# Low-rank rows out of the value products: wider matmuls, values first in a pair, and a separate add on VectorE

## Chip, cores and metric

One NeuronCore of a Trainium2 chip runs the kernel. The metric is the device time of one execution, in microseconds; less is better. TensorE is called PE in the rows, VectorE DVE, ScalarE ACT, GpSimd POOL and SyncE SP.

## Reference, cut to what matters

```python
# x: (8, 256, 1024) fp32; LoRA rank R = 16, scaling 2
h  = x @ W.T + b + 2 * (x @ A[slot]) @ Bm[slot]        # per batch its own slot
q, k, v = h @ w_q, h @ w_k, h @ w_v                    # 32 query heads, 8 kv heads, head dim 32
o  = softmax(q k^T / sqrt(32)) v                       # each kv head serves 4 query heads
x  = x + o @ w_o
y  = x @ weight[id].T                                  # per batch its own 1024 x 1024
logits = y @ router_w.T;  gates = softmax of the top 2 of 4
x  = x + 4 * sum_e gates_e * (y @ A_e.T) @ B_e.T       # rank 16 each
```

## The kernel before

Precision: a product in fp32 is made of three matmuls in the format fp32r. Each operand is split into a high part (written by ScalarE as a rounded copy) and a low part (VectorE subtracts the high part from the original), and high x high, high x low and low x high are summed in PSUM.

Three stages follow one another, each with code for every engine.

The **fold** stage (`fold_stage`) multiplies W into the q, k and v weights, so that attention can be computed from x directly; the folded weights stand in `wq`, twelve blocks of 128 columns in the order of `BLOCKS`, high and low parts. It also folds the low-rank factor B and the bias into `b_scratch` and `bb_scratch`.

The **attend** stage (`attend_stage`) takes the batches in four **pairs**. A pair has 16 **steps** (`STEPS`), one for each kv head and batch, numbered n over all pairs (step 0 to 15 within one). In step n TensorE does, in this order: the scores of n, first two of four tiles (psS, L801); the work of **part 0**; outputs of n-3 (psO: probs times values at L825, row sums with p_sum at L829); the turning of the maxima (psM, L836); transposed scores of n-2, first two (psT, L812); the last two score tiles of n; the work of **part 1**; the last two transposed tiles of n-2. VectorE reduces each score tile to maxima (L673), splits them (L679, L681), and SyncE carries them as two rows into `q_stack`, where they are subtracted inside the transposed scores. ScalarE does the exps (L600), copies outputs (`o_sb`, L608) and GpSimd adds the two halves of probs into p_sum (L550).

The **work** is the projection of x into q, k and v. It fills the parts by a table written by hand, `WORK`; an entry such as `q3:0-4` is a **unit** and the range of 128-row tiles of x that it multiplies (three matmuls of 512 columns each, L759), and a + belongs to the next pair. A q or k unit ends with a low-rank matmul (L766) of `b_stack` with `u_stack`, which holds x times the low-rank factor A of each batch. That product is the unit `u`: 32 matmuls of 256 columns a pair (L740, L742), its parts added on VectorE and split. The value units v0 to v3 (one for each 128 tokens) have 24 matmuls of 256 columns (L774) and one low-rank matmul (L776).

The units go alternately into the two banks of `psP` in the order of `SEQ`. `free` makes a unit wait until the unit two before it has been read: by ScalarE (a q unit: four copies of 32 rows at L566; a value unit: one copy at L587) and by VectorE (a q or k unit: four subtractions, its lows, L653). In a step ScalarE works in the order: maxima rows, two exps, o_sb, units that ended in part 0, values that ended in part 1, two exps, splits of x, q or k units that ended in part 1. VectorE: two maxima, low parts of x (L432), units that ended in part 1 of the step before, two maxima and their split, units that ended in part 0. A q unit also needs its high rows doubled by a DMA (SyncE, L479) before its scores.

The x of the next pair is loaded in steps 11 and 12 as the last unit, q7, lets its tiles go (`x_used`), split by ScalarE in steps 11 (six tiles) and 12 (two), and by VectorE in steps 12 (six) and 13 (two).

The **finish** stage (`finish_stage`) multiplies by w_o and the second weight and computes the gated low-rank part. Its weights are loaded into blocks of `wq` during the last pair.

## Time and profile before

| | |
|---|---|
| median of 3 runs | 1053.18 us (1052.08 to 1053.78) |
| the profiled execution | 1050.59 us, span 1048.9 us |
| mean granted TensorE clock | 0.988 of full |
| TensorE busy | 1013.4 us, 97% |
| VectorE, ScalarE, GpSimd busy | 60%, 43%, 22% |
| fold, to the first value of attention | 0 to 162.5 us |
| a pair in the middle | 288.2 to 422.6 us |

The profiled execution is one run with its own time; the median is of other runs. A busy TensorE can still work at the lower of its two clock levels, so the granted clock is read beside the busy share.

### The profile page before, as it was taken

To read this page: it belongs to the slowest core of one execution; us is meant where nothing else is said; L and a number is where in the kernel's file an instruction comes from. 1 tells how busy PE (TensorE), PEld (TensorE's weight loads), DVE (VectorE), ACT (ScalarE), POOL (GpSimd) and SP (SyncE) were. 2 spreads that over 40 slices of the span, in tenths; PEclk is the share of its full clock that TensorE was granted. 3 is DMA by queue.
4 is the path that set the end of the run, shared out by engine and by line. 5 is a ranking of instruction groups with operands and counts; after the bars stand their busy time and mean duration, and the time that the engine had idled before them with its cause. 6 is when DMAs were issued, how large, how long until landed. Compare 5 with 4: busy or idle time off the path is not lost.

```text
span 1048.9 us, 17421 instructions
## 1 busy us (share of the span) xinstructions
PE 1013.4 (97%) x6934; PEld 820.2 (78%) x6934; DVE 633.5 (60%) x1071; ACT 449.5 (43%) x782; POOL 234.0 (22%) x224
## 2 busy tenths in 40 slices
PE   7999999999999999999999999999899999999997
PEld 6878787877678776787767787676589998988986
DVE  6562724667856578664776657654665655655653
ACT  5121223355754557554665556635422332323321
POOL 1000001123323233223332246643111111111100
PEclk9999999999999999999999999999999999999998
DMA  7030312111421124211232134453966756766531
GB/s 263 0 101 1 131 47 73 27 38 43 123 55 38 29 56 122 60 40 27 53 113 60 42 93 142 123 154 142 257 215 197 229 193 199 228 196 205 201 122 40
DMA packets 49888, 117.41 MB, mean 112 GB/s; under 512 B 7298, under 2 KB 26114, under 8 KB 45712
## 3 DMA queue, kind: packets, MB, share of 16 engines
q1 hardware_dynamic: 40080, 81.70, 26.4%
q0 software_dynamic: 9728, 34.61, 10.4%
q8 instruction: 55, 0.90, 0.4%
q14 instruction: 25, 0.20, 0.1%
HBM read 86.38 MB, written 18.89 MB: 100 GB/s over the span
## 4 chain that ended last, share of the span: by engine, by line
PE 90%; DMA 3%; DVE 3%; ACT 1%; SPq 1%; issue 1%; POOL 0%; ACTq 0%
PE psP L759 20%; PE psW L1043 17%; PE psF L254 11%; PE psG L1071 8%; PE psO L825 6%; PE psT L812 5%; PE psS L801 5%; PE psP L774 4%; PE psX L1286 3%; PE psO L829 2%; PE psY L1305 2%; PE psF L265 1%; DMA x_raw<-in_xT 1%; PE psM L836 1%; PE psP L740 1%; PE psP L742 1%
## 5 line engine op out<-in xcount | busy, mean ns | idle before, releaser
L673 DVE TENSOR_REDUCE nmax<-psS 128x2 f32<-128x512 f32 x256 | 164.5, 684 | 153.8 <-PE psS L801 152.1
L550 POOL TENSOR_TENSOR p_sum<-probs 128x512 f32<-128x512 f32 x128 | 167.6, 1310 | 372.6 <-ACT probs L600 372.3
L759 PE MATMUL psP<-x_hl,wq 128*128 128x512 f32 x960 | 235.1, 392 | 0.6 <-DVE q_stack L653 0.6
L759 PEld LDWEIGHTS psP<-x_hl,wq 128*128 128x128 f32 x960 | 175.2, 189 | 32.8 <-issue 0.8
L1043 PE MATMUL psW<-wq 128*128 128x256 f32 x1536 | 196.7, 283 | 1.6 <-DVE q_stack L653 1.2
L1043 PEld LDWEIGHTS psW<-wq 128*128 128x128 f32 x1536 | 190.3, 191 | 6.2 <-issue 1.3
L600 ACT ACTIVATE probs<-psT 128x512 f32<-128x512 f32 x256 | 139.2, 596 | 54.4 <-PE psT L812 53.9
L1052 ACT ACTIVATE cond_hi<-cond_raw 128x1024 fp32r<-128x1024 f32 x64 | 66.8, 1057 | 152.5 <-PE psG L1071 148.1
L1056 DVE TENSOR_TENSOR cond_lo<-cond_raw,cond_hi 128x1024 fp32r<-128x1024 f32 x64 | 78.3, 1235 | 89.1 <-ACT cond_hi L1052 89.0
L812 PE MATMUL psT<-q_stack,k_stack 98*128 98x512 f32 x256 | 90.1, 427 | 7.7 <-ACT probs L600 5.4
L653 DVE TENSOR_TENSOR q_stack<-psP,q_stack 32x512 fp32r<-32x512 f32 x128 | 87.8, 686 | 9.2 <-ACT q_stack L566 7.1
L801 PEld LDWEIGHTS psS<-k_stack,q_stack 96*128 96x128 f32 x512 | 80.0, 190 | 12.7 <-DVE nmax L673 1.1
L615 ACT ACTIVATE nmax_rows<-psM 16x128 f32<-16x128 f32 x64 | 17.1, 267 | 169.6 <-PE psM L836 169.6
L1003 POOL DMA_DIRECT2D cond_raw<-in_cond x64 | 33.8, 529 | 250.0 <-PE psG L1071 249.9
L801 PE MATMUL psS<-k_stack,q_stack 96*128 96x256 f32 x512 | 85.3, 287 | 0.1
L566 ACT ACTIVATE q_stack<-psP 32x512 fp32r<-32x512 f32 x128 | 75.2, 587 | 9.7 <-PE psP L766 8.1
L254 PE MATMUL psF<-q_hi,w_hi 128*128 128x512 f32 x184 | 72.0, 391 | 2.6 <-DVE bp L217 2.6
L254 PE MATMUL psF<-q_lo,w_hi 128*128 128x512 f32 x184 | 71.7, 389 | 0.0
L254 PE MATMUL psF<-q_hi,w_lo 128*128 128x512 f32 x184 | 71.6, 389 | 0.0
L825 PE MATMUL psO<-probs,v_sb 128*32 128x256 f32 x1024 | 69.3, 388 | 0.0
L812 PEld LDWEIGHTS psT<-q_stack,k_stack 98*128 98x128 f32 x256 | 43.0, 191 | 17.1 <-ACT probs L600 10.7
L825 PEld LDWEIGHTS psO<-probs,v_sb 128*32 128x32 f32 x1024 | 26.9, 110 | 31.5 <-issue 18.1
(122 smaller groups left out, 1252.8 us busy)
## 6 DMA issues: line engine op xcount, KB each, us to landing
cond_raw<-in_cond POOLq DMA_DIRECT2D x64, 512.0 KB, 4.1
x_raw<-in_xT SPq DMA_DIRECT2D x32, 256.0 KB, 3.9
q_stack<-q_stack SPq DMA_DIRECT2D x32, 256.0 KB, 3.1
o_scratch<-o_sb SPq DMA_DIRECT2D x64, 128.0 KB
o_raw<-rden_scratch SPq DMA_DIRECT2D x32, 256.0 KB, 5.4
o_raw<-o_scratch SPq DMA_DIRECT2D x8, 1024.0 KB, 8.8
x_sb<-in_xT SPq DMA_DIRECT2D x8, 1024.0 KB, 6.8
outT<-x_sb SPq DMA_DIRECT2D x32, 256.0 KB, 2.5
```

What stands on the lines that cost most here:

```text
L254: mm = pe.matmul(psF[:, bank(j, m)], w[:, k, m * P:(m + 1) * P], q[:, k], start=(k == 0 and i == 0), stop=(k == KT - 1 and i == 2))
L550: pool.tensor_tensor(p_sum[:, heads], probs[:, 0, heads], probs[:, 1, heads], ALU.add).then_inc(sum_done, 1)
L600: nc.scalar.activation(probs[:, i % 2, (i // 2) * 512:(i // 2 + 1) * 512], psT[:, i % 2], ACT.Exp, scale=ATT_SCALE).then_inc(exp_done, 1)
L653: ins = dve.tensor_tensor(to(h), both(psP[32 * h:32 * h + 32, bank(p, u)]), f(hi(h)), ALU.subtract)
L673: dve.tensor_reduce(nmax[:, n % 2, 2 * hp:2 * hp + 2, qt], psS[:, i % 2].rearrange("p (h k) -> p h k", h=2), AX.X, ALU.max, negate=True).t ...
L759: mm = pe.matmul(out, wq[:, i, w, k * P:(k + 1) * P], x[:, k, part], start=(k == 0 and n_ == 0), stop=False)
L801: mm = pe.matmul(psS[:, i % 2, j * T:(j + 1) * T], q_stack[0:96, slot, c, 2 * hp + j, qt * P:(qt + 1) * P], k_stack[0:96, c, g], start=Tru ...
L812: pe.matmul(psT[:, kt], k_stack[0:98, c, g, kt * P:(kt + 1) * P], q_stack[0:98, slot, c, 2 * hp:2 * hp + 2].rearrange("p h t -> p (h t)"), ...
L825: pe.matmul(psO[HD * h:HD * h + HD, 0], v_sb[:, c, kt, g], probs[:, kt, h * T:(h + 1) * T], start=(kt == 0), stop=(kt == KK - 1))
L1043: mm = pe.matmul(out, wq[:, k, w, m * P:(m + 1) * P], o_part(n % 2, o)[:, k], start=(k == 0 and i == 0), stop=(k == KT - 1 and i == 2))
L1056: dve.tensor_tensor(cond_lo[:, r % RAW], cond_raw[:, r % RAW], f(cond_hi[:, r % SPLIT]), ALU.subtract).then_inc(cond_lo_done, 1)
L1071: mm = pe.matmul(psG[0:EC, half], a[:, k], w[:, half * 512:(half + 1) * 512], start=(k == 0 and i == 0), stop=(k == KT - 1 and i == 2))
```

## The change

The factor A of both batches is put beside the value weights. `v_hi` is a new array whose 320 columns for each tile of x are: low and high part of A of batch 1, 256 value columns, high and low part of A of batch 0; `v_lo` holds the low parts of the value weights. A value matmul takes the value columns and the 32 columns of A of its own batch (288 columns; 272 for the low part of x, 256 for `v_lo`), so that the product of x and A falls out with tokens on the partitions. VectorE adds its two halves into `u_tok` (a reduce for each of v0 to v3), four transposes (unit `t`) turn it, and ScalarE and VectorE write `u_stack` from there. The unit u is gone.

The values must now come first in a pair, so the order of `SEQ` and the table change. The low-rank part of the values, which needs `u_stack`, becomes two units of two matmuls (`r0`, `r1`), which VectorE adds onto `v_sb` in SBUF. `v_sb` exists twice, since the values of a pair are written while the pair before still reads its own. Places in SBUF are moved, the last eight tiles of the fold are evacuated in two pieces, the loads of Wo come up to one step later, and the splits of x are shared out anew over the steps.

```diff
-BLOCKS = ["k0", "q0", "q1", "q2", "v0", "v1", "q3", "k1", "q4", "q5", "q6", "q7"]
+BLOCKS = ["k0", "q0", "q1", "q2", "q3", "k1", "q4", "q5", "q6", "q7", "v0", "v1"]
...
 WORK = [
-    (["v0"], ["q2:0-4"]),
-    (["q2:4-6"], ["q2:6-8"]),
-    (["v1"], ["v2"]),
-    (["v3"], ["q3:0-4"]),
-    (["q3:4-8"], ["k1:0-4"]),
-    (["k1:4-8"], ["q4:0-3"]),
+    (["r0", "r1"], ["q2:0-3"]),
+    (["q2:3-6"], ["q2:6-8"]),
+    (["q3:0-2"], ["q3:2-5"]),
+    (["q3:5-8"], ["k1:0-2"]),
+    (["k1:2-4"], ["k1:4-6"]),
+    (["k1:6-8"], ["q4:0-3"]),
     (["q4:3-6"], ["q4:6-8"]),
     (["q5:0-3"], ["q5:3-5"]),
-    (["q5:5-8"], ["q6:0-3"]),
-    (["q6:3-6"], []),
-    (["q6:6-8"], ["q7:0-3"]),
-    (["q7:3-6"], []),
+    (["q5:5-8"], ["q6:0-2"]),
+    (["q6:2-4"], ["q6:4-6"]),
+    (["q6:6-8"], ["q7:0-2"]),
+    (["q7:2-4"], ["q7:4-6"]),
     (["q7:6-8"], []),
-    (["+u:0-4"], ["+u:4-8"]),
-    (["+k0"], ["+q0"]),
-    (["+q1:0-4"], ["+q1:4-8"]),
+    (["+v0:0-4", "+v1:0-4"], ["+v0:4-8", "+v1:4-8"]),
+    (["+v2", "+v3"], ["+t", "+k0"]),
+    (["+q0"], ["+q1"]),
 ]
-SEQ = ["u", "k0", "q0", "q1", "v0", "q2", "v1", "v2", "v3", "q3", "k1", "q4", "q5", "q6", "q7"]
+SEQ = ["v0", "v1", "v2", "v3", "t", "k0", "q0", "q1", "r0", "r1", "q2", "q3", "k1", "q4", "q5", "q6", "q7"]
...
     def scalar(act):
...
+        def copy_t(p):
+
+            act.wait_ge(proj_done, unit(p, "t") + 1)
+            nc.scalar.activation(u_stack[0:32], psP[0:32, bank(p, "t")], ACT.Copy, scale=LORA_SCALE)
+            nc.scalar.activation(u_stack[32:64], psP[0:32, bank(p, "t")], ACT.Copy, scale=LORA_SCALE).then_inc(proj_act, 1)
...
-                for k in {11: range(0, 6), 12: range(6, KT)}.get(s, ()):
+                for k in {11: range(0, 3), 12: range(3, KT)}.get(s, ()):
                     split_x_hi(act, p + 1, k)
...
     def vector(dve):
...
+            if u[0] == "v":
+
+                c, rows = j // 2, NKV * (1 - j // 2)
+                dve.wait_ge(proj_act, act_unit(p, u) + 1)
+                if p and j == 0:
+                    dve.wait_ge(proj_done, unit(p - 1, "t") + 1)
+                dve.tensor_reduce(u_tok[:, j, c], psP[:, bank(p, u), rows:rows + 2 * R].rearrange("p (h r) -> p r h", h=2),
+                                  AX.X, ALU.add).then_inc(proj_dve, 1)
+            elif u == "t":
+                dve.wait_ge(proj_act, act_unit(p, "t") + 1)
+                dve.scalar_tensor_tensor(u_stack[64:96], psP[0:32, bank(p, u)], LORA_SCALE, f(u_stack[0:32]),
+                                         ALU.mult, ALU.subtract).then_inc(proj_dve, 1)
+            elif u[0] == "r":
+                values = v_sb[p % 2][:, j].rearrange("p k g d -> p (k g d)")
+                dve.wait_ge(proj_done, unit(p, u) + 1)
+                dve.wait_ge(proj_act, act_unit(p, f"v{2 * j + 1}") + 1)
+                dve.tensor_tensor(values, values, psP[:, bank(p, u)], ALU.add).then_inc(proj_dve, 1)
...
-                for k in {12: range(0, 6), 13: range(6, KT)}.get(s, ()):
+                for k in {12: range(0, 3), 13: range(3, KT)}.get(s, ()):
                     split_x_lo(dve, p + 1, k)
-            for unit_ in evacuated(n - 1, 1) if n else [(0, "q1")]:
-                if unit_[1] != "u":
+            for unit_ in finished(n - 1, 1) if n else [(0, "q1")]:
+                if unit_[1][0] in "qk":
+                    evacuate(*unit_)
+            for unit_ in finished(n, 0):
+                if unit_[1][0] not in "qk":
                     evacuate(*unit_)
...
     def tensor(pe):
...
+        def turn_rows(p):
+            free(p, "t")
+            pe.wait_ge(proj_dve, unit(p, "v3") + 1)
+            for t in range(TILES):
+                mm = pe.transpose(psP[0:32, bank(p, "t"), t * P:(t + 1) * P],
+                                  u_tok[:, t].rearrange("p c r -> p (c r)"), id_sb[:])
+            mm.then_inc(proj_done, 1)
...
+        def project_v(p, t, first, end):
+
+            c, toks = t // 2, slice(t * P, (t + 1) * P)
+            if first == 0:
+                free(p, f"v{t}")
+                if t == 0:
+                    pe.wait_ge(a_lo_done, p + 1)
+            out = psP[:, bank(p, f"v{t}")]
+            hi_rows, lo_rows, lo_out = ((slice(V0, VC), slice(V0, VC - R), slice(0, NKV + R)) if c == 0 else
+                                        (slice(0, VC - V0), slice(R, VC - V0), slice(R, NKV + V0)))
+            for k in range(first, end):
+                if t == 0:
+                    pe.wait_ge(x_lo_done, KT * p + k + 1)
+                pe.matmul(out[:, 0:NKV + V0], x[:, k, 0, toks], v_hi[:, k, hi_rows], start=(k == 0), stop=False,
+                          skip_group_check=True)
+                pe.matmul(out[:, lo_out], x[:, k, 1, toks], v_hi[:, k, lo_rows], start=False, stop=False,
+                          skip_group_check=True)
+                mm = pe.matmul(out[:, c * V0:c * V0 + NKV], x[:, k, 0, toks], v_lo[:, k], start=False, stop=(k == KT - 1),
+                               skip_group_check=True)
+            if end == KT:
+                mm.then_inc(proj_done, 1)
+
+        def low_rank_v(p, c):
+            free(p, f"r{c}")
+            for t in range(2):
+                toks = slice(c * T + t * P, c * T + (t + 1) * P)
+                mm = pe.matmul(psP[:, bank(p, f"r{c}"), t * NKV:(t + 1) * NKV], u_stack[:, toks],
+                               b_stack[:, VB * P:(VB + 2) * P], start=True, stop=True)
+            mm.then_inc(proj_done, 1)
```

On TensorE, at the start of pair 0: the last q unit (q1), the first scores, and what follows. Before:

```order
L766 MATMUL psP<-u_stack,b_stack 128x512
L801 MATMUL psS<-k_stack,q_stack 128x256 x4
L774 MATMUL psP<-wq,x_hl 128x256 x24
L776 MATMUL psP<-b_stack,u_stack 128x256
L801 MATMUL psS<-k_stack,q_stack 128x256 x4
L759 MATMUL psP<-x_hl,wq 128x512 x12
```

Now:

```order
L791 MATMUL psP<-u_stack,b_stack 128x512
L851 MATMUL psS<-k_stack,q_stack 128x256 x4
L819 MATMUL psP<-b_stack,u_stack 128x256 x4
L851 MATMUL psS<-k_stack,q_stack 128x256 x4
L784 MATMUL psP<-x_hl,wq 128x512 x9
```

The 24 matmuls of v0 stood between the two groups of scores; the four of r0 and r1 stand there now.

On VectorE, steps 12 and 13 of pair 0, from the first maxima of step 12 to the second of step 13. Before:

```order
L673 TENSOR_REDUCE nmax<-psS 128x2 [waits s_done] x2
L432 TENSOR_TENSOR x_hl<-x_raw,x_hl 128x512 [waits x_hi_done] x6
L673 TENSOR_REDUCE nmax<-psS 128x2 [waits s_done] x2
L679 CAST nmax_parts<-nmax 128x8 [waits s_max]
L681 TENSOR_TENSOR nmax_parts<-nmax,nmax_parts 128x8 [waits nmax_hi]
L653 TENSOR_TENSOR q_stack<-psP,q_stack 32x2x256 [waits half_hi]
L653 TENSOR_TENSOR q_stack<-psP,q_stack 32x2x256
L653 TENSOR_TENSOR q_stack<-psP,q_stack 32x2x256 [waits proj_act]
L653 TENSOR_TENSOR q_stack<-psP,q_stack 32x2x256
L673 TENSOR_REDUCE nmax<-psS 128x2 [waits s_done] x2
L432 TENSOR_TENSOR x_hl<-x_raw,x_hl 128x512 [waits x_hi_done] x2
```

Now:

```order
L703 TENSOR_REDUCE nmax<-psS 128x2 [waits s_done] x2
L452 TENSOR_TENSOR x_hl<-x_raw,x_hl 128x512 [waits x_hi_done] x3
L703 TENSOR_REDUCE nmax<-psS 128x2 [waits s_done] x2
L709 CAST nmax_parts<-nmax 128x8 [waits s_max]
L711 TENSOR_TENSOR nmax_parts<-nmax,nmax_parts 128x8 [waits nmax_hi]
L672 TENSOR_TENSOR q_stack<-psP,q_stack 32x2x256 [waits half_hi]
L672 TENSOR_TENSOR q_stack<-psP,q_stack 32x2x256
L672 TENSOR_TENSOR q_stack<-psP,q_stack 32x2x256 [waits proj_act]
L672 TENSOR_TENSOR q_stack<-psP,q_stack 32x2x256
L703 TENSOR_REDUCE nmax<-psS 128x2 [waits s_done] x2
L452 TENSOR_TENSOR x_hl<-x_raw,x_hl 128x512 [waits x_hi_done] x5
```

Three low parts of x have moved from ahead of q7's lows to behind them and behind the next maxima.

On TensorE, from part 1 of step 8 to part 0 of step 9 and its outputs (the step behind the end of q5). Before:

```order
L759 MATMUL psP<-x_hl,wq 128x512 x9
L812 MATMUL psT<-q_stack,k_stack 128x512 x2
L801 MATMUL psS<-k_stack,q_stack 128x256 x4
L759 MATMUL psP<-x_hl,wq 128x512 x9
L825 MATMUL psO<-probs,v_sb 32x256 x8
L829 MATMUL psO<-p_sum,ones 32x256 x4
```

Now:

```order
L784 MATMUL psP<-x_hl,wq 128x512 x6
L862 MATMUL psT<-q_stack,k_stack 128x512 x2
L851 MATMUL psS<-k_stack,q_stack 128x256 x4
L784 MATMUL psP<-x_hl,wq 128x512 x6
L875 MATMUL psO<-probs,v_sb_82 32x256 x8
L879 MATMUL psO<-p_sum,ones 32x256 x4
```

Both blocks of projection ahead of the outputs are six matmuls long instead of nine.

## Rows read from the trace of the kernel before

**Rows 1.** The page: its first line, and the busy time of each engine.
```profile
span 1048.9 us, 17421 instructions
PE 1013.4 (97%) x6934; PEld 820.2 (78%) x6934; DVE 633.5 (60%) x1071; ACT 449.5 (43%) x782; POOL 234.0 (22%) x224
```

**Rows 2.** Groups by line, whole run: busy us, mean ns, idle before.
```profile
L774 PE MATMUL psP<-wq,x_hl 128*128 128x256 f32 x384 | 48.6, 283 | 0.0
L587 ACT ACTIVATE v_sb<-psP 128x256 f32<-128x256 f32 x16 | 6.3, 395 | 8.1 <-PE psP L776 8.1
```

**Rows 3.** Chain of waits: start, us on the chain, what.
```profile
204.05 2.87 PE psP L774 x24
...
289.08 5.46 PE psP L759 x24
```

**Rows 4.** Waits of TensorE, 160 to 700 us: total, times, longest.
```profile
PE psT L812 <- ACT probs L600: 5.4, 3, 2.3
```

**Rows 5.** Timeline, TensorE, step 13 of pair 0: start, us, what.
```profile
286.11 0.28 PE L740 MATMUL psP<-x_hl,a_stack 128*64 128x256 f32 x1
...
287.96 0.64 PE L812 MATMUL psT<-q_stack,k_stack 98*128 98x512 f32 x2
```

**Rows 6.** Timeline, first scores of pair 0 and what follows.
```profile
183.53 0.71 PE L801 MATMUL psS<-k_stack,q_stack 96*128 96x256 f32 x4
...
184.04 1.29 DVE L673 TENSOR_REDUCE nmax<-psS 128x2 f32<-128x512 f32 x2 [2.15 <-PE psS L801]
...
185.36 2.79 DVE L653 TENSOR_TENSOR q_stack<-psP,q_stack 32x512 fp32r<-32x512 f32 x4
...
188.29 2.08 PE L759 MATMUL psP<-x_hl,wq 128*128 128x512 f32 x8 [0.58 <-DVE q_stack L653]
```

**Rows 7.** Timeline, steps 10 and 11 of pair 0; q6 has ended in step 10.
```profile
262.95 0.65 PE L801 MATMUL psS<-k_stack,q_stack 96*128 96x256 f32 x4
...
264.36 2.40 ACT L566 ACTIVATE q_stack<-psP 32x512 fp32r<-32x512 f32 x4
...
265.62 2.79 DVE L653 TENSOR_TENSOR q_stack<-psP,q_stack 32x512 fp32r<-32x512 f32 x4
...
266.79 1.09 ACT L600 ACTIVATE probs<-psT 128x512 f32<-128x512 f32 x2
...
267.95 1.28 POOL L550 TENSOR_TENSOR p_sum<-probs 128x512 f32<-128x512 f32 x1 [2.59 <-ACT probs L600]
...
268.57 1.07 PE L825 MATMUL psO<-probs,v_sb 128*32 128x256 f32 x16
...
269.46 0.61 PE L829 MATMUL psO<-p_sum,ones 128*32 128x256 f32 x8
...
270.04 0.71 PE L812 MATMUL psT<-q_stack,k_stack 98*128 98x512 f32 x2
...
270.59 0.65 PE L801 MATMUL psS<-k_stack,q_stack 96*128 96x256 f32 x4
...
271.20 0.19 PEld L812 LDWEIGHTS psT<-q_stack,k_stack 98*128 98x128 f32 x1 [0.18 <-ACT probs L600]
...
271.52 0.60 ACT L608 ACTIVATE o_sb<-psO 128x512 f32<-128x512 f32 x1
...
272.72 1.56 PE L759 MATMUL psP<-x_hl,wq 128*128 128x512 f32 x6
```

**Rows 8.** Timeline, VectorE, start of step 13 of pair 0.
```profile
283.35 1.29 DVE L673 TENSOR_REDUCE nmax<-psS 128x2 f32<-128x512 f32 x2
...
284.56 1.28 DVE L432 TENSOR_TENSOR x_hl<-x_raw,x_hl 128x512 fp32r<-128x512 f32 x2
```

**Rows 9.** The page, DMA issues: KB each, us from issue to landing.
```profile
q_stack<-q_stack SPq DMA_DIRECT2D x32, 256.0 KB, 3.1
```

**Rows 10.** Stretches: length, busy us by engine; last three: granted clock, DMA share, GB/s.
```profile
280.70:284.10 3.40, 3.40 (x25) 2.35 (x27) 3.33 (x6) 3.11 (x6) 1.21 (x1) 0.50 0.41 77
...
550.30:553.70 3.40, 3.40 (x23) 2.57 (x25) 3.30 (x6) 3.31 (x7) 0.99 (x1) 0.50 0.40 77
```

More of the change, by code:

```diff
@@ L65, in placer, with fold_stage @@
     return at
[L68 removed]
+def fold_stage(nc, sem, at, ctx, wq, v_hi, v_lo, id_sb, idx_sb, ones, W, Wqkv, bias, lora_BT, ident, idx, idx2_sb, idx2,
                b_scratch, bb_scratch):
@@ L318, in finished, with act_unit, attend_stage @@
     return [(p, u) for p, u, _, end in work(n, part) if end == KT]
-def evacuated(n, part):
-    if part:
-        return finished(n, 1)
-    late = [(p, u) for p, u in finished(n - 1, 0) if u == "v0"] if n else []
-    return late + [(p, u) for p, u in finished(n, 0) if u != "v0"]
 def unit(p, u):
     return NS * p + SEQ.index(u)
-def dve_unit(p, u):
-    return ND * p + SEQ_DVE.index(u)
-def attend_stage(nc, sem, at, ctx, wq, id_sb, idx_sb, ones, nmax, nmax_parts, before, ahead, xT, lora_A, b_scratch,
+def act_unit(p, u):
+    return NA * p + SEQ_ACT.index(u)
+def attend_stage(nc, sem, at, ctx, wq, v_hi, v_lo, id_sb, idx_sb, ones, nmax, nmax_parts, before, ahead, xT, lora_A, b_scratch,
                  bb_scratch, oT, den_scratch, rden_scratch):
@@ L395, in bank, with factor @@
         return unit(p, u) % 2
+    def factor(c, low):
+        i = (NKV + V0 + low * R) if c == 0 else (1 - low) * R
+        return slice(i, i + R)
     def pair_rows(scratch, p):
@@ L766, in project @@
                 pe.matmul(out, b_stack[:, i * P:(i + 1) * P], u_stack[:], start=False, stop=True).then_inc(proj_done, 1)
-        def project_v(p, t):
-            free(p, f"v{t}")
-            i = BLOCKS.index("v0")
-            out, toks = psP[:, bank(p, f"v{t}"), 0:NKV], slice(t * P, (t + 1) * P)
-            for k in range(KT):
-                for n_, (w, part) in enumerate(((0, 0), (0, 1), (1, 0))):
-                    pe.matmul(out, x[:, k, part, toks], wq[:, i:i + 2, w, k * P:(k + 1) * P],
-                              start=(k == 0 and n_ == 0), stop=False)
-            pe.matmul(out, u_stack[:, toks], b_stack[:, i * P:(i + 2) * P], start=False, stop=True).then_inc(proj_done, 1)
+        def project_v(p, t, first, end):
[18 more added lines that the diff above has]
+                mm.then_inc(proj_done, 1)
@@ L958, in ahead_sync @@
         if s == 8:
-            sp.wait_ge(before.proj_done, unit(PAIRS - 1, "q5") + 1)
+            sp.wait_ge(before.proj_done, unit(PAIRS - 1, "v3") + 1)
             for i in range(2):
```

234 lines of the change are left out of this document (113 added, 121 removed).

## Prediction, made blind

> **What bounds the kernel now.** I read the page first. TensorE is busy for 97% of the span [rows 1], so I take it as the bound and ask two things: what work of TensorE goes, and where TensorE will stand still that it did not before. The groups by line give the durations of one operation [rows 2], the chain of waits the true spacing of matmuls in a stream [rows 3], and the timeline shows, around four places, who waits for whom. The reader should see that TensorE works through its program almost without gaps: from 160 to 700 us its waits for ScalarE sum to 5.4 us [rows 4], all in one place, the end of a pair. The other engines lie close behind it, in places by only 0.2 us. So the order of the work counts as much as its amount.
>
> All times below are of the profiled execution, 1050.6 us with a span of 1048.9. The median of the runs is 1053.2, 2.6 above it, and I add that at the end.
>
> **The work that goes.** In a pair, 32 matmuls of the low-rank product (L740, L742) go. Sixteen take 1.85 us from the first to the score matmul behind them [rows 5], 0.116 each, so 3.7 us. The value products stay 24 to a tile, but 8 x (288 + 272 + 256) = 6528 columns instead of 6144. A run of 24 takes 2.87 us at 256 columns and 5.46 at 512 [rows 3]: 2.59 us for 6144 columns more, so 384 columns cost 0.16 us, and four tiles 0.65. Four transposes of 128 columns come in, at most 0.12 each by the 256-column spacing, 0.45. The four low-rank matmuls of the values only move. Sum: -3.7 + 0.65 + 0.45 = -2.6 us a pair, **-10.4 us** in four. New work of VectorE (four small reduces, two adds) and ScalarE (one copy less) counts only where TensorE waits for it.
>
> **Step 0 of every pair: r0, r1.** psP has two banks, and a unit may start when the unit two before it has been read. Before, v0 stood behind the first scores and needed only q0's bank; q2 needed q1's. The start of pair 0 shows what q1's bank costs [rows 6]: scores start at 183.53, VectorE's maxima at 184.04, q1's low parts follow until 188.15, and q2 starts at 188.29, 4.76 us after the scores. TensorE had 3 us of v0 in between and still waited 0.58. Now r1 needs q1's bank, and ahead of it stand only the scores (0.5) and r0 (0.25). It waits 4.76 - 0.75 = 4.0 us, four times, less the 0.6 of today: **+15.4 us**. Nothing can cover it: outputs, scores and q2 are queued behind r1.
>
> **Step 13: v0 waits for x.** VectorE now makes three of the low parts of x in step 12 and five in step 13 (six and two before), and v0:0-4 needs the first four. The fourth comes behind, on VectorE: maxima and their split, q7's four low parts, and the next two maxima. The pattern up to q7's lows is that of q6 [rows 7]: scores at 262.95, lows from 265.62 to 268.41, so +5.5 us. Two maxima take 1.3 [rows 8] and one x part 0.64 (two in 1.28, [rows 8]): +7.4. TensorE gets there earlier: from these scores to the next block of work are 2.1 us where nothing lies between (270.59 to 272.72, [rows 7]), and the nine matmuls on the first three tiles take about 1.1, so +3.2. The wait is 4.2 us, three times, 12.6. The data are not late: x's transfers start in step 11 as before. The 5.4 us of waits for ScalarE go [rows 4]: these were exps queued on ScalarE behind six splits of x, some of them waiting for a transfer, and now three splits stand there. **+7.2 us.**
>
> **Step 14: t waits for v3.** The transposes need v2 and v3 copied by ScalarE and reduced by VectorE. ScalarE comes to v2 only after the two exps and o_sb, which wait for the transposed scores: those start at 270.04, o_sb ends at 272.12 [rows 7], +2.1. Two copies of 0.395 us [rows 2] and a reduce of some 0.2 make +3.1; TensorE is free at +1.0, after the scores of 270.59. The wait is 2.1 us, three times. In pair 0 nothing stands ahead of the copy: 0.9. **+7.2 us.**
>
> **Step 15.** q0 ends one step later than before, and is doubled by a DMA that takes 3.1 us [rows 9]. ScalarE's copies begin 2.1 us after the transposed scores (behind o_sb), last 2.4 (264.36, [rows 7]), then the DMA: +7.6; TensorE, with q1 (5.7) between, is there at +7.2. 0.5 us, three times: **+1.5 us.**
>
> **Steps 4, 9, 11: the row sums.** These follow a step in which q3, q5 or q6 ends. The order is: four copies (264.36), then two exps (266.79), then GpSimd's sum until 269.23, which TensorE's matmul on p_sum needs; it started at 269.46, with 0.23 us to spare [rows 7]. From the scores of 262.95 that is 6.51 us, of which two blocks of 9 matmuls are 4.1. In the new table these blocks are 6 and 6, 1.37 us less. The chain over ScalarE and GpSimd keeps its 6.3 us, so TensorE waits 1.1 us, in part ahead of the probs matmuls. Three a pair, twelve in all: **+13.2 us.** In return parts 1 of steps 9 and 11, empty before, are filled, and the waits there of some 0.4 us (0.18 shown, and its like on the second tile, [rows 7]) go eight times: **-3.2 us.** Here is the surprise of the table: it spreads the work more evenly, and takes the reserve away where it was needed.
>
> **The clock.** The granted clock is 0.50, the 1.2 GHz level, for 3.4 us after the wait at each of the pair ends (280.7 the first, 550.3 the third) [rows 10]; such a stretch does 1.7 us of work, so it costs 1.7. Three in the transitions now. The new waits of 4.0 and 4.2 us are longer than any of these, so I give each a stretch (7), and the three of 2.1 two more: nine, six above today, **+10.2 us**. The Trainium skill ("TensorE: Matmul & The Clock Gate", section on HAM oscillation) says that a kernel whose matmuls are cut by waits pays the fall again at every one, "Every single K-tile". By it each of the ten new waits of 2 to 4 us would pay, seven above today, +11.9, a total 1.7 higher.
>
> **Sum:** -10.4 + 15.4 + 7.2 + 7.2 + 1.5 + 13.2 - 3.2 + 10.2 = +41.1 us, 1091.7 for a profiled execution, **1094 us** for the median.
>
> The fold stage pays nothing: its last eight tiles are copied and subtracted in two pieces, but v0 needs only tiles and x parts that VectorE has done before the bias matmul ends, give or take 0.5 us. The finish stage moves only addresses and one load of Wo.
>
> **Unknown costs.** The reduce of a 128x32 tile out of PSUM is not in the trace; it is 0.2 us if it is like the small ones, 0.68 if like a 128x512, which would add 0.5 to four waits: 0 to +2. The clock: with falls for the long waits only in part, +3; with one for every wait down to the 1.1 us, up to +25, though these are broken in two and shorter than anything that went with a fall. Row sums: 0 if ScalarE runs ahead, 13.2 if not, and in the last pair, where GpSimd splits Wo too, perhaps 3 more.
>
> **The rivals.** *Fewer waits than I count*: the clocks fall only as often as today and the row-sum waits vanish. For it: every row-sum chain has parts that could start sooner when TensorE has just been held up. Against: each of these chains starts at a matmul of TensorE itself, so lateness doesn't shorten it. -13.2 and up to -10.2: +18 to +28, 1071 to 1081.
>
> *Faster*: TensorE is the bound and arrives late everywhere, so the waits are covered as q2's nearly is today, where only 0.58 remains [rows 6]. Then -10.4, -3.2, the 5.4 us gone, and the three falls of the clock with them, 5.1: 24 us less, 1029. For it: the page's 97%. It decides once the new waits and their clock stay under 24 us together; I count 65. Against it: r1's is read off pair 0 almost directly, and alone with its clock it is 22. A partial form would end between 1045 and 1055.
>
> *Slower still*: SyncE or the transfers add a wait. The shortest steps now hold two blocks of 1.37 us, and in them the rows of the maxima must be copied, issued and landed (a q_stack transfer takes 3.1 us, [rows 9]) before the transposed scores. +5 to +15: 1099 to 1109.
>
> **The numbers.** My forecast (1084 to 1099) 0.5; fewer waits (1065 to 1084) 0.27; slower still 0.13; faster 0.06, a partial form near no change 0.04 (0.01 faster, 0.02 the same, 0.01 slower). A measurement of this kernel can tell 0.2%, 2.1 us. Range 1068 to 1103: it leaves out most of the last two and the end of slower still. Faster 0.07, same 0.02, slower 0.91.
>
> **What the new profile would show.** PE waits for DVE at the low-rank matmuls r1, four times 4 us; at the first 288-column matmul on the fourth x tile, three times some 4 us, with x_hl as releaser; at the transposes, three times 2 us; at p_sum, twelve times about 1 us with POOL or ACT as releaser. The value products 3.05 us for 24. The granted clock 0.5 in some nine stretches between 160 and 700. A pair of 134.4 us grows to about 145. Prediction wrong: if the r1 wait is under 1 us, VectorE gets to q1's lows in another order than I read; if p_sum never waits, the spare time is larger than the one place that I measured it at.

## The result and the profile after

The changed kernel takes **1102.05 us** (median of 4 runs, 1100.35 to 1103.01), against 1052.63 for the kernel before in runs beside it: a ratio of 1.047, 95% interval 1.0449 to 1.0491. The profiled execution took 1103.01 us with a span of 1101.2, 52.3 us above the span of [rows 1]. The forecast of 1094 was right in direction and 8 us low; the time lies 1 us inside the upper end of the range, 1103.

The page of the changed kernel, its first line and the busy time of each engine, against [rows 1]:

```profile
span 1101.2 us, 17254 instructions
PE 1021.1 (93%) x6822; PEld 818.7 (74%) x6822; DVE 637.4 (58%) x1099; ACT 448.4 (41%) x786; POOL 231.3 (21%) x224
```

TensorE runs 112 matmuls fewer and is busy 7.7 us longer, and its share falls from 97% to 93%. Both point the same way: less work, done in part at the lower clock, with more time standing still. No other engine grew by more than 4 us. The waits of TensorE from 160 to 745 us (what stood still <- what released it: us in total, times, longest), against [rows 4]:

```profile
PE psP L819 <- DVE q_stack L672: 15.3, 4, 3.8
PE psP L806 <- DVE x_hl L452: 12.0, 3, 4.0
PE psO L875 <- ACT probs L618: 11.6, 11, 1.8
PE psP L768 <- DVE u_tok L683: 6.2, 4, 1.8
PE psT L862 <- DMA q_stack<-nmax_rows: 5.4, 1, 5.4
PE psO L879 <- POOL p_sum L569: 3.6, 12, 0.5
PE psW L1094 <- DVE q_stack L672: 1.1, 1, 1.1
PE psS L851 <- issue: 1.0, 3, 0.4
```

L819 is r1, L806 v0's first product, L768 the transposes of t, L875 and L879 the output matmuls, L862 the transposed scores. All of these together are 56.2 us. In the kernel before, the same view down to the first psW matmul adds up to 10.6. The three waits that the change was predicted to bring to single places have their number and their size: four of 3.8, three of 4.0, three of 1.8 and one of 0.8.

How r1 comes to wait, in the timeline of all engines at the start of pair 1 (start, us, what; in brackets the idle time before it and its releaser):

```profile
335.44 0.71 PE L851 MATMUL psS<-k_stack,q_stack 96*128 96x256 f32 x4 [0.35 <-issue]
...
335.95 1.29 DVE L703 TENSOR_REDUCE nmax<-psS 128x2 f32<-128x512 f32 x2 [2.19 <-PE psS L851]
...
337.27 2.78 DVE L672 TENSOR_TENSOR q_stack<-psP,q_stack 32x512 fp32r<-32x512 f32 x4
340.09 0.69 DVE L693 TENSOR_TENSOR v_sb<-v_sb,psP 128x512 f32<-128x512 f32 x1
...
340.20 0.77 PE L819 MATMUL psP<-b_stack,u_stack 98*128 98x256 f32 x2 [3.81 <-DVE q_stack L672]
```

This is [rows 6] again, 152 us later: scores, maxima, q1's four low parts until 340.05, then r1 at 340.20, 4.76 us after the scores, as read blind from pair 0 of the kernel before. VectorE's own addition for r0 (340.09) starts after the parts of q1 and has nothing to do with the wait.

The wait that the prediction sized by the wrong rule is that of step 4, which stands four times in the row of L875. ScalarE and TensorE there, in pair 0:

```profile
219.62 0.60 ACT L626 ACTIVATE o_sb<-psO 128x512 f32<-128x512 f32 x1
221.21 2.41 ACT L583 ACTIVATE q_stack<-psP 32x512 fp32r<-32x512 f32 x4 [0.98 <-PE psT L862]
223.64 1.08 ACT L618 ACTIVATE probs<-psT 128x512 f32<-128x512 f32 x2
```

```profile
220.54 0.63 PE L862 MATMUL psT<-q_stack,k_stack 98*128 98x512 f32 x2
...
221.48 1.52 PE L784 MATMUL psP<-x_hl,wq 128*128 128x512 f32 x6
224.78 1.07 PE L875 MATMUL psO<-probs,v_sb 128*32 128x256 f32 x16 [1.77 <-ACT probs L618]
```

ScalarE has q3 to copy and stands idle for 0.98 us until transposed scores (L862, 220.54) have run. q_stack has three slots, and q3's is still being read by the scores of q0. Two exponentials are queued behind the four copies, and the outputs need them. From start to start the outputs are 1.84 us late here, and 0.72 us late in steps 9 and 11, where no copy waits for a slot: the difference, 1.1 us, is about the 0.98 us that ScalarE stood idle.

The granted clock in two stretches (length, PE busy, clock, DMA share, GB/s), against [rows 10]:

```profile
339.82:343.23 3.41, 3.03 (x26) 0.50 0.20 43
438.81:445.64 6.83, 5.55 (x35) 0.50 0.06 20
```

The first begins 0.38 us before r1 of pair 1 starts, near the end of its wait, the second 1.28 us before the end of the x wait of the next transition (435.80 to 440.09). From 160 to 745 us there are twelve such stretches with 54.6 us in all, where the kernel before has four of 3.4 us up to the same point. To price one, I took for each matmul in it the distance to the next start, less the median distance of the same two instructions at the full clock, and left waits out. A stretch of 3.4 us costs 1.1 to 1.7 us, one of 6.8 us 2.0 to 2.6. The twelve cost 20.6 us, the four before 5.9. These prices are estimates: with other groups of instructions for the medians the sums come out up to 1.3 us higher.

### The profile page after: what moved, and what is told of

Its sections match the earlier page's. It is cut to its first block, busy times and chain, and to the rows that moved or that the text cites. A ratio compares the mean times of both kernels' runs of the same rounds, so it can differ in the third digit from the quotient of the medians.

```text
span 1101.2 us, 17254 instructions
## 1 busy us (share of the span) xinstructions
PE 1021.1 (93%) x6822; PEld 818.7 (74%) x6822; DVE 637.4 (58%) x1099; ACT 448.4 (41%) x786; POOL 231.3 (21%) x224
## 4 chain that ended last, share of the span: by engine, by line
PE 84%; ACT 5%; DVE 5%; DMA 2%; POOL 1%; issue 1%; SPq 0%; ACTq 0%; DVEq 0%
PE psP L784 18%; PE psW L1094 16%; PE psF L274 11%; PE psG L1122 8%; PE psO L875 5%; PE psT L862 5%; PE psS L851 4%; PE psO L879 3%; PE psX L1337 3%; ACT q_stack L583 2%; ACT probs L618 2%; DVE q_stack L672 2%; PE psP L806 2%; PE psY L1356 2%; PE psP L808 1%; POOL p_sum L569 1%
## 5 line engine op out<-in xcount | busy, mean ns | idle before, releaser
L784 PE MATMUL psP<-x_hl,wq 128*128 128x512 f32 x960 | 245.8, 402 | 0.0
L784 PEld LDWEIGHTS psP<-x_hl,wq 128*128 128x128 f32 x960 | 179.6, 195 | 32.8
L862 PE MATMUL psT<-q_stack,k_stack 98*128 98x512 f32 x256 | 88.4, 425 | 5.4 <-DMA q_stack<-nmax_rows 5.4
L851 PEld LDWEIGHTS psS<-k_stack,q_stack 96*128 96x128 f32 x512 | 80.7, 193 | 14.5 <-issue 2.8
L875 PE MATMUL psO<-probs,v_sb 128*32 128x256 f32 x1024 | 73.6, 408 | 11.6 <-ACT probs L618 11.6
L875 PEld LDWEIGHTS psO<-probs,v_sb 128*32 128x32 f32 x1024 | 27.8, 114 | 46.1 <-issue 18.6
L862 PEld LDWEIGHTS psT<-q_stack,k_stack 98*128 98x128 f32 x256 | 44.1, 195 | 12.1 <-DMA q_stack<-nmax_rows 5.6
```

The lines of the kernel that those rows point to most:

```text
L784: mm = pe.matmul(out, wq[:, i, w, k * P:(k + 1) * P], x[:, k, part], start=(k == 0 and n_ == 0), stop=False)
L851: mm = pe.matmul(psS[:, i % 2, j * T:(j + 1) * T], q_stack[0:96, slot, c, 2 * hp + j, qt * P:(qt + 1) * P], k_stack[0:96, c, g], start=Tru ...
L862: pe.matmul(psT[:, kt], k_stack[0:98, c, g, kt * P:(kt + 1) * P], q_stack[0:98, slot, c, 2 * hp:2 * hp + 2].rearrange("p h t -> p (h t)"), ...
L875: pe.matmul(psO[HD * h:HD * h + HD, 0], v_sb[p % 2][:, c, kt, g], probs[:, kt, h * T:(h + 1) * T], start=(kt == 0), stop=(kt == KK - 1))
```

## The experiments

All are edits of the changed kernel, but for the sixth. Each was timed in three or five rounds beside the kernel before, which gave medians of 1054.34 (experiments 1 to 4), 1052.42 (5 to 8) and 1051.56 us (9 to 11). Since these shift by some us, gains that are added up are taken from the ratios. Spans are those of the profiled executions.

**1. r1 one part of a step later.**

```diff
-    (["r0", "r1"], ["q2:0-3"]),
+    (["r0"], ["r1", "q2:0-3"]),
```

> The changed kernel with r1 moved from part 0 of step 0 to part 1, ahead of q2; nothing else. My theory (each wait is a chain of its own that begins at a matmul of TensorE, so what is taken away comes back in full): outputs, transposed scores and two score tiles, some 2.5 us, now lie between r0 and r1 in three pairs, and only the score tiles, 0.5 us, in pair 0. The waits at the low-rank value matmuls fall from 15.3 us to about 8, with 2 to 3 us of the clock: 1092 to 1094 us against 1102. Rival theory (VectorE is the true limit around the start of a pair, and a wait that goes at one place comes back at the next): the wait moves to q2 or to the scores of step 1, and the time is 1099 to 1102.

1092.6 us (1090.1 to 1096.44), ratio 1.038 [1.034, 1.0421]. Waits of TensorE, 160 to 745 us:

```profile
PE psP L806 <- DVE x_hl L452: 12.0, 3, 4.0
...
PE psP L819 <- DVE q_stack L672: 5.4, 4, 2.4
```

9.9 us of the r1 wait are gone, and the time fell by 9.5, as expected. It did not come back as a wait at one place, which the rival needs: all waits in this view fell from 56.2 to 47.6 us. But the low clock up to the end of the pairs also costs some 5 us less, so the 9.5 (10.3 in the span) are less than the two together. Some 3 us did come back, about 1 of them as low clock in the last stage, the others in distances too short for the view of waits.

**2. Four parts of x in step 12.**

```diff
-                for k in {12: range(0, 3), 13: range(3, KT)}.get(s, ()):
+                for k in {12: range(0, 4), 13: range(4, KT)}.get(s, ()):
```

(and the same on ScalarE, one step earlier)

> The changed kernel with the splits of x shared out 4 and 4 over the two steps instead of 3 and 5, on ScalarE and VectorE; nothing else. My theory: v0:0-4 then has its four tiles before it starts; the wait for x_hl falls from 12.0 us to under 2, and the three falls of the clock behind it (4.4 us together) go too: 1086 to 1090 us. Rival theory (the time comes back at the next wait, since VectorE has the same work ahead of the second maxima of step 13): waits for x_hl or for the maxima in part 1 of step 13, 1097 to 1102 us.

1091.27 us (1088.96 to 1094.42), ratio 1.0369 [1.0332, 1.0407]. The row of x_hl, 12.0 us, is gone. In its place stands

```profile
PE psP L806 <- DVE q_stack L672: 5.0, 3, 1.7
```

which is v1, waiting for the bank of q7: 12.0 us given, 5.0 taken back, and the clock's share on top. The time is 1 us above the range that I had put on record.

**3. ScalarE copies the value tiles ahead of its exponentials.**

```diff
             more = n < N and p + 1 < PAIRS
+            for unit_ in finished(n, 0):
+                if unit_[1][0] == "v":
+                    evacuate(*unit_)
             if 1 <= n <= N:
                 act.wait_ge(turned, n)
...
             for unit_ in finished(n, 0):
-                evacuate(*unit_)
+                if unit_[1][0] != "v":
+                    evacuate(*unit_)
```

> The changed kernel with ScalarE copying v2 and v3 at the start of step 14, ahead of the maxima rows and the two exps instead of behind them and o_sb; nothing else. My theory: the copies are done while TensorE works on outputs, the wait at the transposes falls from 6.2 us to about 0.9 (pair 0 alone), and three falls of the clock (4.6 us) go: 1091 to 1094 us. Rival theory (ScalarE only shifts the delay to its exps): the transposed scores behind k0 wait instead, 1099 to 1102 us.

1093.53 us (1090.96 to 1095.05), ratio 1.0384 [1.0349, 1.0419]. The wait for u_tok falls from 6.2 us to 0.8, which is pair 0's alone. The other waits of the pairs stay; the last pair's wait for nmax_rows grows from 5.4 to 6.4 us.

**4. Parts of nine matmuls again.**

```diff
-    (["q3:0-2"], ["q3:2-5"]),
-    (["q3:5-8"], ["k1:0-2"]),
-    (["k1:2-4"], ["k1:4-6"]),
-    (["k1:6-8"], ["q4:0-3"]),
+    (["q3:0-2"], ["q3:2-4"]),
+    (["q3:4-6"], ["q3:6-8"]),
+    (["k1:0-2"], ["k1:2-5"]),
+    (["k1:5-8"], ["q4:0-3"]),
...
-    (["q5:5-8"], ["q6:0-2"]),
-    (["q6:2-4"], ["q6:4-6"]),
-    (["q6:6-8"], ["q7:0-2"]),
-    (["q7:2-4"], ["q7:4-6"]),
+    (["q5:5-8"], ["q6:0-3"]),
+    (["q6:3-6"], []),
+    (["q6:6-8"], ["q7:0-3"]),
+    (["q7:3-6"], []),
```

> The changed kernel with the table changed so that blocks of nine matmuls follow the end of q5 and of q6 as before the change, and q3 ends in part 1 of step 3 instead of part 0; parts 1 of steps 9 and 11 are empty again. My theory: TensorE's waits at probs and at p_sum (15.2 us) go nearly all, some 3 us of waits for exps in the two empty parts come back, 1 to 2 us of the clock go: 1087 to 1091 us. Rival theory (the waits at probs are set by the total of the work in a pair, not by where the blocks stand): at most 4 us, 1098 to 1102.

1092.32 us (1090.25 to 1093.18), ratio 1.037 [1.0337, 1.0402]. Of 15.2 us of waits for probs and p_sum 1.1 remain, while the wait for nmax_rows grows from 5.4 to 7.8 us; the time is 1 us above the expected range. But this edit does two things at once, and experiments 10 and 11 take them apart.

**5. Matmuls in place of the wait.** The kernel waits just as long for r1's bank, but TensorE is kept busy meanwhile. The result of the added matmuls is read by nothing.

```diff
         def low_rank_v(p, c):
+            if c == 1:
+                for i in range(32):
+                    pe.matmul(psM[:, P:P + NKV], wq[:, 0, 0, (i % KT) * P:(i % KT + 1) * P], v_lo[:, i % KT],
+                              start=True, stop=True)
             free(p, f"r{c}")
```

> The changed kernel, with 32 matmuls of 256 columns added ahead of the wait for r1's bank (their result, in a part of PSUM that nothing reads, is used nowhere, so they only keep TensorE busy for 32 x 0.12 = 3.8 us, about as long as the wait of 3.75 us). My theory: TensorE's idleness is what brings the stretches of 0.5 clock that follow r1 (starts at 196, 340, 490 and 637 us, costing 2.1, 0.24, 0.23 and 1.5 us of matmul time). r1 itself starts no later than now, those four stretches go, and the time falls by about 4 us, to 1098 us (1095 to 1101). Rival 1, the low clock follows from something else than the idle time (the place in the program, VectorE's or ScalarE's work): the stretches stay and the time is 1102 or, if the added matmuls run past the wait, some tenths per pair above. Rival 2, the whole excess over the waits (some 12 us) hangs on the first fall in each pair: the time falls by 8 us or more.

1093.71 us (1093.01 to 1096.73), ratio 1.0388 [1.0362, 1.0415]: 8.3 us less, twice what I expected. The timeline of TensorE in pair 1 and the clock of the stretch that holds the added matmuls (length, busy us of PE, PEld, DVE, ACT, POOL, clock, DMA share, GB/s):

```profile
331.99 0.40 PE L823 MATMUL psP<-b_stack,u_stack 98*128 98x256 f32 x2
332.23 4.00 PE L818 MATMUL psM<-v_lo,wq 128*128 128x256 f32 x32
336.21 0.47 PE L823 MATMUL psP<-b_stack,u_stack 98*128 98x256 f32 x2
```

```profile
333.50:336.90 3.40, 3.40 (x33) 3.02 (x36) 3.33 (x6) 0.75 (x2) 0.00 (x0) 1.00 0.36 77
```

From the second matmul of r0 to r1 are 4.10 us (332.11 to 336.21), and 4.09 without the added matmuls (336.11 to 340.20), so nothing was gained on the wait itself. No r1 is followed by a stretch of low clock any more, while in the changed kernel and in experiments 2, 3, 4, 10 and 11, which leave the wait of 3.8 us as it is, all four are. Of twelve stretches six are left, and their cost falls from 20.6 to 11.4 us, enough for the 8.3. The four stretches that follow an r1 cost 1.98, 1.12, 1.28 and 2.5 = 6.9 us, more than the 4.1 that I had put on record, since I had undercounted the output matmuls in them. Two more stretches (at 312.5 after the t wait of the first transition, and at 374.0 after a q3 wait, 2.9 us) didn't occur in this execution, and one after an x wait lasted twice as long, 1.1 us more. Of rival 2, that everything hangs on the first fall, no more than that is true: the x waits still fall, all three.

**6. The kernel before, with q6 and q7 in sixes.**

```diff
-    (["q5:5-8"], ["q6:0-3"]),
-    (["q6:3-6"], []),
-    (["q6:6-8"], ["q7:0-3"]),
-    (["q7:3-6"], []),
+    (["q5:5-8"], ["q6:0-2"]),
+    (["q6:2-4"], ["q6:4-6"]),
+    (["q6:6-8"], ["q7:0-2"]),
+    (["q7:2-4"], ["q7:4-6"]),
```

> The kernel before, with one part of the change done alone: q6 and q7 dealt out as two k-tiles per part of a step in steps 8 to 11, where it had three and then a part with none. My theory (the row sums' term of the prediction): with two k-tiles between them, TensorE reaches the output matmuls of steps 9 and 11 before the last exponentials of probs, 8 waits of about 1.1 us = 8.8 us, while the parts that no longer are empty give back about 3.2 us: 5.6 us more, ratio 1.005 (1.003 to 1.008), and waits for probs or p_sum rise from 6.5 to some 12 to 15 us. Rival 1, these waits in the changed kernel came from other work that moved with them: no change, ratio within 0.998 to 1.002. Rival 2, the clock falls at these waits as well: ratio above 1.009.

1052.22 us (1049.8 to 1054.9), ratio **0.9995** [0.998, 1.0011]. My theory expected 1.005 and missed. The waits did appear:

```profile
PE psO L825 <- ACT probs L600: 5.2, 8, 0.7
PE psT L812 <- ACT probs L600: 4.4, 3, 1.6
PE psO L829 <- POOL p_sum L550: 3.1, 10, 0.6
```

and they have the predicted size. One place, in pair 0:

```profile
268.29 1.07 PE L825 MATMUL psO<-probs,v_sb 128*32 128x256 f32 x16 [0.65 <-ACT probs L600]
269.65 0.64 PE L829 MATMUL psO<-p_sum,ones 128*32 128x256 f32 x8 [0.28 <-POOL p_sum L550]
```

The view has 0.65 and 0.28 us; from start to start, against the usual distances, it is 0.72 and 0.46, 1.18 together, where 1.1 was forecast. What the prediction sized too low is what the filled parts give back. The starts of the psM transposes, one a step, tell the net price of this dealing. They are subtracted here from one another for pair 2, from step 8 on:

```
                 turn to turn, us             sum of four
before           7.64  5.87  7.64  5.86       27.01
in sixes         7.49  6.50  7.49  6.50       27.98
```

That is 0.97 us a pair, 3.9 in four. Two waits of 1.18 are 2.36 a pair, so the filled parts give back 1.4, where the forecast had 0.8. Against the 3.9, this execution has two stretches of low clock in place of four up to the end of the pairs, 3.3 us less. Whether that is the new dealing or chance stays open: over all runs the mean granted clock is 0.9886 (12 runs) against 0.9867 (18 runs of the kernel before), some 2 us, which is not clear of their scatter. What the runs bound is the whole: at most 1.2 us more.

**7. r0 and r1 where their bank is long free.** q2 goes ahead, and both low-rank products use q1's bank, with counters of their own; q3, the next unit of that bank, waits for the second addition.

```diff
-    (["r0", "r1"], ["q2:0-3"]),
-    (["q2:3-6"], ["q2:6-8"]),
+    (["q2:0-2"], ["q2:2-4", "r0"]),
+    (["q2:4-6", "r1"], ["q2:6-8"]),
...
-            free(p, f"r{c}")
+            if c:
+                pe.wait_ge(low_added, 2 * p + 1)
+            else:
+                pe.wait_ge(proj_act, act_unit(p, "q1") + 1)
+                pe.wait_ge(proj_dve, unit(p, "q1") + 1)
...
             if first == 0:
                 free(p, u)
+                if u == "q3":
+                    pe.wait_ge(low_added, 2 * p + 2)
```

> The changed kernel, with the two low-rank products of the values put where the bank they write is long free: q2 goes ahead of them, r0 in the second part of step 0 and r1 in the first part of step 1, both in q1's bank, with counters of their own. My theory: the r1 wait (15.3 us over four pairs) goes altogether, not just the 9.9 us of the first experiment, and with it the 4 us of low clock that follow it: 1085 us (1081 to 1090), and the largest waits left on psP are u_tok's 6.2 and x_hl's 12.0. Rival, VectorE's lateness (the copies of q1 and q2 and the added sums stand in the same row) only shows up at the next bank, q3's, or at the outputs of step 3: 1090 us or more, with a wait at q3 or ahead of the outputs of some 1 to 2 us each.

1078.61 us (1076.81 to 1081.02), ratio 1.023 [1.0204, 1.0255]. Waits of TensorE, 160 to 748 us:

```profile
PE psP L809 <- DVE x_hl L453: 12.0, 3, 4.0
...
PE psP L826 <- DVE q_stack L673: 0.8, 1, 0.8
```

23.4 us less for one edit: 14.5 of the r1 wait (0.8 remain, at r0 of pair 0), 7.6 of the clock (20.6 to 13.0). That is 2.4 us beyond the low end of what I expected, and again the clock was worth more than I had put on it.

**8. All four repairs (edits 2, 3, 4 and 7).**

> The changed kernel with all four repairs at once: r0 and r1 apart, x_hl in four and four, the copies of v ahead of the exponentials, and the parts of nine matmuls. My theory (the losses are separate waits that add up): 1102 less 17, 11, 8.5 and 10 = about 1055.5 us (1050 to 1061), ratio to before 0.998 to 1.008; waits left inside the pairs: q7's bank ahead of v1 (5.0) and the last pair's nmax_rows (5 to 8). Rival 1, the change's saving of 10.4 us comes through once its waits are gone: 1040 to 1047 us, ratio 0.988 to 0.995. Rival 2, the repairs overlap (each removes a bit of the same lateness): 1062 us or more, ratio above 1.009.

1046.25 us (1045.91 to 1051.83), ratio **0.994** [0.992, 0.9961]: 0.6% below the kernel before. My estimate (1050 to 1061) missed; the time lies in the range of rival 1. Waits of TensorE, 160 to 748 us, those of the pairs:

```profile
PE psT L873 <- DMA q_stack<-nmax_rows: 5.5, 1, 5.5
PE psP L813 <- DVE q_stack L677: 5.2, 3, 1.8
PE psT L873 <- ACT probs L619: 1.6, 2, 1.3
PE psW L1105 <- DVE q_stack L677: 1.2, 1, 1.2
PE psO L890 <- POOL p_sum L570: 1.1, 1, 1.1
PE psS L862 <- issue: 1.0, 3, 0.4
PE psP L830 <- DVE q_stack L677: 0.8, 1, 0.8
PE psP L773 <- DVE u_tok L688: 0.8, 1, 0.8
PE psS L862 <- DVE nmax L708: 0.7, 2, 0.5
```

They sum to 17.9 us, 7.3 above the kernel before. The low clock up to the end of the pairs costs 3.7 against 5.9 there, 2.2 less. With the -10.4 of work that the prediction counted, this makes -5.3 us. Its span is 1044.2, 4.7 below [rows 1]. So the balance closes with the work at the figure that was counted, within 1 us.

**9. The last pair's transfers.** Experiment 8, with o_raw's 1 MB from o_scratch issued a step later than the four transfers of rden_scratch.

```diff
-        sp.dma_start(o_land(n % 2), oT[n]).then_inc(o_landed[n % 2], 16)
+        if n:
+            sp.dma_start(o_land(n % 2), oT[n]).then_inc(o_landed[n % 2], 16)
...
             load_o(sp, 0)
+        if s == 9:
+            sp.dma_start(o_land(0), oT[0]).then_inc(o_landed[0], 16)
```

> The kernel with all repairs (1046.3 us), with one change of the last pair's transfers: o_raw's 1 MB from o_scratch is issued one step later than the four transfers of rden_scratch, and not right behind them. My theory: the rows of nmax that TensorE waits 5.5 us for in the last pair (2.3 in the kernel before) land late because 2 MB of o_raw stand on the 16 engines ahead of them; with half of it a step later that wait shrinks to 0 to 2 us and the 6.8 us stretch of low clock that follows it (2.2 us) goes: 1039 to 1042 us, ratio to before 0.988 to 0.991. Rival, the late rows come from the transfer of wo_raw or from SyncE's order, or the second half now delays the next step's rows: a wait of 3 to 5 us stays, in the same or the next step, and the time is 1045 to 1047 us.

1048.92 us (1046.33 to 1051.04), ratio 0.9975 [0.996, 0.999]. My estimate missed and the rival held, with a time 2 us above its range: the rows of the maxima are as late as before, and a new wait stands beside them, with a second stretch of low clock.

```profile
PE psT L873 <- DMA q_stack<-nmax_rows: 5.3, 1, 5.3
...
PE psS L862 <- DVE nmax L708: 3.8, 4, 2.5
```

So the half that was moved is not what delays them. What stayed ahead of them are wo_raw's transfer and the four of rden_scratch. Which of these it is was not tried. The profiles point at wo_raw, without showing it: in the kernel before and in experiment 6 no wo_raw is issued in that step, and from the issue of the rows to the transposed scores are 7.4 us; in the other eleven profiles its 512 KB are issued 2.4 to 3.1 us ahead of the rows, and it is 10.0 to 12.2 us.

**10. q3 late, nothing else.** Steps 2 to 5 of edit 4 alone.

> The changed kernel, with steps 2 to 5 alone dealt as in the fourth experiment, so that q3 ends in the second part of step 3 and not in the first; steps 8 to 11 stay in sixes. My theory, which departs from the prediction's row sums: the wait of step 4 (1.8 to 1.9 us, against 0.8 in steps 9 and 11) is not one of a short part, but of q3's copies on ScalarE, which stand ahead of two exponentials and wait for the slot of q_stack until the step's last score tiles are read. From turn to turn of the maxima, steps 2 to 4 of a pair take 23.0 us in the changed kernel and 20.7 with q3 late: 4 x 2.3 = 9.3 us less, with a stretch of low clock 10 us, 1092 us (1090 to 1095), and the rows of probs and p_sum fall from 15.2 to about 7 us. Rival, the prediction's own view (all twelve waits are alike, 1.1 us each): four of them go, 4 to 5 us less, 1097 to 1098 us.

1091.59 us (1087.26 to 1100.55), ratio 1.0389 [1.0354, 1.0423].

```profile
PE psO L875 <- ACT probs L618: 4.5, 7, 0.6
PE psO L879 <- POOL p_sum L569: 2.4, 8, 0.5
```

From 15.2 us to 6.9, and 10.5 us less time by the medians, 8.5 by the ratios. The prediction's view, in which all twelve waits are alike, would have given 4 to 5.

**11. Nines in steps 8 to 11, nothing else.**

> The changed kernel, with steps 8 to 11 alone dealt in nines again; q3 ends in the first part of step 3 as in the change. My theory: from turn to turn, a pair of such steps takes 14.0 us in sixes and 13.5 in nines, so 8 x 0.49 = 3.9 us less before any change of the clock: 1098 us (1096 to 1101), with some 7 us of the waits for probs and p_sum gone and 3.2 us paid for parts that are empty. Rival, the prediction's view (8 waits of 1.1 us, less 3.2 of empty parts): 5.6 us less, 1096.5 us. Rival 2, as in the kernel before with sixes (ratio 0.9995): nothing that can be told, 1102 us.

1099.41 us (1097.6 to 1100.79), ratio 1.045 [1.0431, 1.0468]: 2.6 us less by the medians, 2.1 by the ratios. With experiment 10 this makes up the fourth one (0.0081 and 0.002 of the ratio, against 0.010).

```profile
PE psO L875 <- ACT probs L618: 7.1, 4, 1.8
PE psO L879 <- POOL p_sum L569: 2.2, 5, 1.1
```

The turns of steps 8 to 11 take the 7.64 and 5.86 us of the kernel before, so 3.9 us were gained there. The last pair's wait for nmax_rows grew from 5.4 to 7.6 us, which takes 2.2 back. The prediction's view (5.6 us) is above all of these.

## Why the prediction was right, point by point

The direction and the main waits were right. The size was right in part by luck: 1102 lies outside the 1084 to 1099 of the forecast's main case and 1 us inside the range. By its number it falls to *slower still*, but that rival's mechanism, late transfers, has only 3.1 us of added wait and 2.0 of clock.

**r1, +15.4.** Measured 15.3 less the 0.6 of q2 that went: +14.7, 3.8 us a time for 4.0. Read off pair 0 of the kernel before, it was nearly exact. Experiments 1 and 7 show that it is q1's bank, that VectorE's order sets it, and that nothing covers it.

**v0 and the fourth part of x, +7.2.** Measured 12.0 less 5.4 that went: +6.6. Experiment 2 shows the cause, and what is late next, q7's bank, which the prediction did not name.

**t, +7.2.** Measured 6.2. Experiment 3 shows the cause.

**q0's transfer, +1.5.** The score matmuls ahead of the next step 0 start 0.5 us late (334.70 to 335.44, where 0.23 us is the usual distance). The view gives 1.0 us for three. No experiment was made on it.

**Row sums, +13.2 and -3.2.** Net, the forecast had 10.0; from turn to turn it is 3.9 us for steps 9 and 11 and 9.3 for step 4 (against q3 late), 13.2 in all, and two errors pull against each other. For steps 9 and 11 the wait of 1.1 us was right (1.18 from start to start), but the term "-3.2" for the filled parts was too small: they give back some 5.6, so that these steps cost 3.9 net and not 5.6. The step that failed is to count step 4 among "Three a pair, twelve in all", all at 1.1 us. It has another cause on top, a q_stack slot that is still read, and is 1.84 us late ahead of the probs and 0.46 at p_sum, 2.3 from start to start. Experiment 10 puts 8.5 to 10.5 us on it with its clock, where its share was four waits of 1.1, 4.4 us. The prediction noticed which step q3 ends in and took it for a short part like the others. What it left out is that ScalarE's copy of q3 waits for the slot that the transposed scores of the same step still read.

**The clock, +10.2.** Measured +14.7 up to the end of the pairs: twelve stretches against four, where the forecast had nine against three. This term is the largest miss of the sum. Eight more in place of six is one part. The other is length: four of the twelve last 6.8 us and cost up to 2.6, where the forecast took 3.4 us and 1.7 for each. By the Trainium skill ("TensorE: Matmul & The Clock Gate", section on HAM oscillation) each of the ten new waits was to pay, and all ten are followed by a stretch: the rule agrees with this trace, and its total, 1.7 us above mine, was the nearer one. The page's own case is of longer waits, for transfers; here three of the ten, t's, are 1.8 us long. "Every single" wait of that length is not what the runs show: of the four waits for probs in step 4, 1.8 us each, one is followed by a stretch, and in experiment 5 one of t's three is not. The rule also leaves out the two other stretches, after a q3 wait and after the late rows of the maxima. Experiment 5 shows that the idle time is the cause, since the same program at the same place, with matmuls in the wait, has no fall there.

**Work, -10.4.** Experiment 8 closes with it to 0.6 us (-5.3 by the terms, -4.7 in the span).

**Missed: the last pair's rows of the maxima.** In the kernel before, the view of [rows 4] has

```profile
PE psT L812 <- DMA q_stack<-nmax_rows: 2.3, 1, 2.3
```

and it is 5.4 now, with a stretch of low clock behind it that costs 2.0 us. The prediction had a transfer's lateness as a rival of its own (slower still) and nothing for it in its sum. Experiment 9 did not find its cause. Without this wait, the waits would add up to 42.5, under the 44.5 of the forecast: that the two totals agree so well is luck.

**The sum.** Waits +45.6 (forecast 44.5), clock +14.7, work -10.4, filled parts -3.2, the last stretch of the kernel (742.7 to the end, 358.5 us against 357.1) +1.4: +48.1 of the 52.3 measured, with work and filled parts as forecast. The 4.2 left over are what the view of waits and the prices above leave out: from start to start the gaps are 0.1 to 0.2 us longer than the view has them (4.17 for the 4.0 of x, 1.98 for the 1.8 of t, 0.65 for the 0.5 of p_sum), and there are more than thirty. A count over all distances between starts of TensorE closes. From 160 us to the first psW matmul (686.6 us before, 737.6 now, 51.0 more) it has +45.7 for the waits of the view, +3.7 around them, +17.4 for the low clock (now with the distances that hold a wait as well), -12.5 for the instructions at their usual distances and -3.4 for delays too short for the view, those in the parts that were empty above all: +50.9. A pair in the middle grew to 149.8 and 147.5 us, where about 145 was forecast.

**The faster rival** needed the new waits and their clock to stay under 24 us. r1 alone has 15.3 and 6.9 = 22.2 of that, for which the prediction had 22, and the waits for x, for t and at the row sums go far beyond it. But the rival was right in one thing. With these four waits removed or shortened, the changed kernel is 0.6% [0.4, 0.8] faster than the one before, in experiment 8. It lost by its order of work, not by its wider products. Whether the gain is the products' own is not shown: the new shares of the x splits also take away 5.4 us of waits at the pair ends, and no run tries them in the kernel before alone.

## What to carry to other kernels

When blocks are moved on the engine that bounds, write down for each moved block which buffer it needs, who reads that buffer last, and what is queued there ahead of that read. The four biggest losses here (a PSUM bank, a split of x, a tile that is copied late, a slot of q_stack) would each stand in such a list. A wait that looks like another one by its length may have another cause: look at what the releaser itself waited for before counting it with its neighbours. And price a wait on TensorE with what follows it: r1's 15.3 us cost some 23 once the clock is counted.

## What the runs showed that was not expected

Keeping TensorE busy through a wait that nothing shortens gave back 8.3 us of 1102 (experiment 5), by the clock alone. Up to the end of the pairs the stretches at the 1.2 GHz level last 3.4 or 6.8 us, with one of 10.2 in each of experiments 1, 2, 7 and 11, and the long ones are not dear in proportion: over all profiled executions 1.6 to 3.0 us against 1.1 to 1.7. And repairs of single waits added up: by the ratios, experiments 2, 3, 4 and 7 alone are worth 0.0101, 0.0086, 0.0100 and 0.0240, in all 0.0527, and together 0.0530. That the two agree so closely is luck, since each ratio is known to 0.002 to 0.004; what they show is that the repairs hardly overlap.
